# A batch's closing chain of attention, done within the two batches behind it

## The reference

```python
x = x + attn_a(layernorm(x))     # linear layer, cumulative sum over the features
x = x + ffn(layernorm(x))        # 8 experts, the 2 best for each token
x = x + attn_b(layernorm(x), ...)
x = x + ffn(layernorm(x))

def attn_b(x, Wq, bq, Wk, bk, Wv, bv, Wo, bo):      # 16 heads of 8 features
    q, k, v = x @ Wq.T + bq, x @ Wk.T + bk, x @ Wv.T + bv
    scores = einsum('bqhd,bkhd->bhqk', q, k) / sqrt(8)
    scores = where((j <= i) & (j >= i - 128), scores, -10000.0)   # i query, j key
    attn = softmax(scores) + 1e-9
    return einsum('bhqk,bkhd->bqhd', attn, v) @ Wo.T + bo
```

## Time and profile before

| | us |
|---|---|
| median of 3 runs | 1003.95 (993.8 to 1005.53) |
| the profiled execution | 1002.63 |
| its span, first to last instruction | 1000.6 |
| PE busy / DVE busy / ACT busy in the span | 686.4 / 645.7 / 407.8 |
| stage of attn_b | about 369 to 716 |
| mean granted clock of PE | 0.865 of full |

### The profile page before, as it was taken

One profiled execution on the slowest core, in us unless ns is written; L12 is line 12 of the kernel. 1 busy time (PEld: TensorE's weight loads), 2 busy tenths in 40 slices (PEclk: granted clock), 3 DMA queues, 4 the chain that ended last, 5 costly groups with the idle time before them and its releaser, 6 DMA issues.

```text
span 1000.6 us, 29220 instructions
## 1 busy us (share of the span) xinstructions
PE 686.4 (69%) x10592; PEld 511.6 (51%) x10592; DVE 645.7 (65%) x2608; ACT 407.8 (41%) x691; POOL 437.5 (44%) x413
## 2 busy tenths in 40 slices
PE   3811777797667677885978879867675668566780
PEld 2511566675546553553545555555465556455660
DVE  7887887864444569764668576777778634354444
ACT  1370245353333332753547447555354234233340
POOL 6591573584655500213031100051486766666661
PEclk9999967999887796997899889987759999789895
DMA  7210012132212220111111101001011111223114
GB/s 223 59 32 3 25 35 67 49 68 56 62 51 85 67 79 26 55 56 37 53 28 60 51 24 58 4 3 44 17 51 49 43 44 41 64 75 104 54 41 137
DMA packets 62921, 54.53 MB, mean 54 GB/s; under 512 B 10129, under 2 KB 55954, under 8 KB 62778
## 3 DMA queue, kind: packets, MB, share of 16 engines
q1 hardware_dynamic: 53250, 33.12, 11.2%
q0 software_dynamic: 9536, 19.55, 7.8%
HBM read 31.79 MB, written 20.84 MB: 53 GB/s over the span
## 4 chain that ended last, share of the span: by engine, by line
PE 38%; DVE 30%; issue 12%; another core or an unknown queue 7%; DVEq 4%; DMA 3%; ACT 3%; SPq 1%; POOL 1%; ACTq 0%; POOLq 0%
PE stbank L1115 6%; DVE sbank L830 4%; PE stbank L1102 4%; PE stbank L1104 3%; PE stbank L1116 3%; DVE gl L770 3%; DVE zr L589 3%; PE bank L1209 3%; PE sbank L1167 2%; PE stbank L1103 2%; DVE ysb L760 2%; DVE st L560 2%; PE stbank L1193 2%; DVE xs L786 2%
## 5 line engine op out<-in xcount | busy, mean ns | idle before, releaser
L479 POOL DMA_INDIRECT xg<-table,idx x156 | 160.5, 1029 | 168.2 <-PE sbank L1083 58.7
L909 ACT ACTIVATE g<-stbank 128x512 f32<-128x512 f32 x156 | 93.3, 598 | 322.0 <-PE stbank L1104 235.6
L1115 PE MATMUL stbank<-wff,gh 128*128 x624 | 142.1, 306 | 112.2 <-DVE ysb L760 70.7
L434 POOL TENSOR_TENSOR r<-ve,mhalf 128x4 f32<-128x4 f32 (+1 forms) x32 | 43.1, 1346 | 305.6 <-DVE ve L566 211.2
L760 DVE TENSOR_REDUCE ysb<-stbank 128x128 f32<-128x256 f32 x156 | 65.9, 422 | 153.2 <-remote 90.4
L1102 PE MATMUL stbank<-xT,wff 128*128 128x128 f16 x624 | 149.6, 247 | 18.1 <-issue 12.3
L1104 PE MATMUL stbank<-xT,wff 128*128 128x128 f16 x624 | 149.8, 247 | 0.5 <-issue 0.4
L1103 PE MATMUL stbank<-xT,wff 128*128 128x128 f16 x624 | 147.2, 243 | 0.0
L956 ACT ACTIVATE pT<-stbank 128x1024 f32<-128x1024 f32 (+1 forms) x128 | 116.6, 915 | 74.2 <-PE stbank L1193 73.9
L1115 PEld LDWEIGHTS stbank<-wff,gh 128*128 128x128 f16 x624 | 67.2, 108 | 145.4 <-issue 128.2
L830 DVE CUSTOM_DVE_ANT_0 sbank<-sbank,mskew 128x160 f32<-128x160 f32 x384 | 113.2, 356 | 27.0 <-PE sbank L1167 26.7
(11 more groups left out here) (187 smaller groups left out, 1366.2 us busy)
## 6 DMA issues: line engine op xcount, KB each, us to landing
yslot<-ysb SPq DMA_DIRECT2D x78, 64.0 KB
table<-tb SPq DMA_DIRECT2D x16, 256.0 KB
cg<-ytab SPq DMA_DIRECT2D x16, 256.0 KB
qz<-dumps SPq DMA_DIRECT2D x96, 32.0 KB
kst<-dumps SPq DMA_DIRECT2D x96, 32.0 KB
xg<-table,idx POOLq DMA_INDIRECT x156
xs<-in_x SPq DMA_DIRECT2D x8, 256.0 KB, 4.9
qz<-in_w SPq DMA_DIRECT2D x1, 2048.0 KB, 10.0
```

The lines of the kernel that those rows point to most:

```text
L479: g.indirect_dma_start(xg[:, i % G].rearrange("p a d -> p (a d)"), None, table[cc % 2], bass.IndirectOffsetOnAxis(ap=idx[:, cc % 2, t:t + ...
L909: a.activation(g32[:, i % 3, :], hbank[i % 2], ACT.Silu, scale=1.0 / WSCALE)
L1115: mm(o, gh[:, i % 3, P * f:P * f + P], whl, start=(f == 0), stop=False, skip_group_check=True)
```

## The change

- `back` is taken apart. Within iteration b, PE transposes `uT` of batch b-1 in slots 3, 7, 11 and 15 (`u_rows`), and DVE's division follows (`context`). The contexts of batch b-2 are transposed in slot 1 (`context_columns`, now into `bank[1]`), copied, and projected in slot 2 (`project`), then added (`add_attention`). What is left of batches 6 and 7 follows the loop.
- The row transposes go to bank 3 of `stbank`. For that the units with kt = 3 put their four heads side by side into one bank, and the band matmuls of kt = 1 and kt = 3 write the whole width, since the mask that had stayed in these banks is overwritten. In units with kt = 1 `scores_t` waits for the division.
- `uT` exists twice, for even and odd batches. The odd ones lie in buffers that the stage does not use otherwise.
- `FRONT_EARLY` is 2 instead of 4: every step of the preparation is two slots later, and batch 2's steps 2 and 3 are done in the loop.
- `max_rows(b, 1)`, which was at the end of the iteration, is in slot 0 of the next. The router's counts for cc = 2 are in `sbank` instead of `bank[1]`. Waits are adapted.

```diff
-FRONT_EARLY = 4
+FRONT_EARLY = 2
+CTX_AT = 1
...
+        uT = [[u_even[:, i, :] for i in range(SETS)],
+              [gh[:].rearrange("p a n -> p (a n)").bitcast(F32)[:, 0:SEQ], gl[:].rearrange("p a n -> p (a n)").bitcast(F32)[:, 0:SEQ],
+               g32[:, 2, :], ysb[:].rearrange("p a n -> p (a n)")]]
...
+        rbank = [bank[1][:, :] if cc != CHUNKS else sbank[:, 1, :] for cc in range(2 * CHUNKS)]
...
+        def u_bank(b, qt):
+            return stbank[:, TPB - 1 if b + 1 < B else qt, :]
...
             for b in range(B):
                 for j in range(UNITS):
                     if b + 1 < B:
                         reduce(b + 1, j)
+                    if j == CTX_AT + 1 and b >= 2:
+                        add_attention(b - 2)
+                    if b and j % TPB == TPB - 1:
+                        context(b - 1, j // TPB)
                     front_in_attention(front, b, j)
                     router_in_attention(r_step, b, j)
-                back(b)
+            add_attention(B - 2)
+            for qt in range(TPB):
+                context(B - 1, qt)
+            add_attention(B - 1)
...
                     if j >= 2:
                         exps(b, j)
+                    if j == 0:
+                        max_copy(b, 1)
+                    if j == CTX_AT and b >= 2:
+                        ctx_copy(b - 2)
...
             def front(b, j):
                 if j == 5:
-                    wait(pe, s_oa, b - 2)
+                    wait(pe, s_oa, b - 3)
...
                 if j == 0 and half == 0:
                     pe.wait_ge(s_stk[b % 2], 16 * 24 * (b // 2 + 1))
-                    wait(pe, s_cx, TPB * (b - 1))
...
                 wait(pe, s_e, UNITS * b + j - 1)
-                halves = 2 if kt < TPB - 1 else 1
-                for half in range(2):
-                    bank_ = stbank[:, 2 * (j % 2) + half, :].rearrange("p (g a n) -> p g a n", g=2, a=2)
+                if b and kt == 1:
+
+                    wait(pe, s_cx, TPB * (b - 1) + j // TPB)
+                w = 256 if kt < TPB - 1 else P
+                flat_ = stbank[:].rearrange("p a n -> p (a n)")[:, 1024 * (j % 2):1024 * (j % 2) + 4 * w]
+                for o in range(0, 4 * w, 512):
                     for c in range(NBLK):
                         r = slice(BLK * c, BLK * c + BLK)
...
+                        if kt in (0, 2):
+                            out_ = flat_[r, o:o + 512].rearrange("p (g a n) -> p g a n", g=2, a=2)[:, :, :, r]
+                            band = mband[:].rearrange("p (a n) -> p a n", a=2)[:, :, r].unsqueeze(1).to_broadcast([P, 2, 2, BLK])
+                        else:
+                            out_ = flat_[r, o:o + 512]
+                            band = mband[:, 0:w].unsqueeze(1).to_broadcast([P, 512 // w, w])
+                        mm(out_, ident16[:, r], band, start=True, stop=False, tile_position=(0, BLK * c), skip_group_check=True)
...
+            def u_rows(b, qt):
+                if qt == 0:
+                    pe.wait_ge(s_u, SETS * (b + 1))
+                dst = u_bank(b, qt)
+                for s in range(SETS):
+                    ins = pe.transpose(dst[:, P * s:P * s + P], uT[b % 2][s][:, P * qt:P * qt + P], ident[:])
+                ins.then_inc(s_ut, 1)
+
+            def context_columns(b, maxima):
+                pe.wait_ge(s_mt, maxima)
+                wait(pe, s_oa, b)
+                pe.wait_ge(s_cx, TPB * (b + 1))
                 for qt in range(TPB):
...
+                    ins = pe.transpose(bank[1][:, P * qt:P * qt + P], cx[:, qt, :], ident[:])
                 ins.then_inc(s_cxp, 1)
...
                         if j >= 2:
                             scores_t(b, j)
+                        if j == 0:
+                            max_rows(b, 1)
+                        if j == CTX_AT and b >= 2:
+                            context_columns(b - 2, 2 * (b + 1))
+                        if j == CTX_AT + 1 and b >= 2:
+                            project(b - 2)
+                        if b and j % TPB == TPB - 1:
+                            u_rows(b - 1, j // TPB)
                         front_in_attention(front, b, j)
...
-                back(b)
+            context_columns(B - 2, 2 * B)
+            project(B - 2)
+            for qt in range(TPB):
+                u_rows(B - 1, qt)
+            context_columns(B - 1, 2 * B)
+            project(B - 1)
```

More of the change, by code:

```diff
@@ L540, in _ @@
             layer_pass(a_step, r_step, x_step, beside, 0)
-            front(2, 2)
             for b in range(B):
@@ L824, in reduce @@
                 if j == 0:
+                    wait(dve, s_mtp, 2 * b - 1)
+                if j == MAX_SPLIT:
                     wait(dve, s_mtp, 2 * b)
@@ L832, in reduce, with context, add_attention @@
                     ins.then_inc(s_red, 1)
-            def back(b):
-                for qt in range(TPB):
-                    dve.wait_ge(s_ut, TPB * b + qt + 1)
-                    u = sbank[:, qt % 2, :].rearrange("p (h r) -> p h r", r=32)
-                    v.reciprocal(rden[:, qt, :], u[:, :, DK])
-                    dve.drain()
-                    v.tensor_tensor(cx[:, qt, :].rearrange("p (h j) -> p h j", j=DK), u[:, :, 0:DK],
-                                    rden[:, qt, :].unsqueeze(2).to_broadcast([P, NH, DK]), ALU.mult).then_inc(s_cx, 1)
+            def context(b, qt):
+                dve.wait_ge(s_ut, TPB * b + qt + 1)
+                if qt == 0:
+                    wait(dve, s_cxp, b)
+                u = u_bank(b, qt).rearrange("p (h r) -> p h r", r=32)
+                v.reciprocal(rden[:, qt, :], u[:, :, DK])
+                dve.drain()
+                v.tensor_tensor(cx[:, qt, :].rearrange("p (h j) -> p h j", j=DK), u[:, :, 0:DK],
+                                rden[:, qt, :].unsqueeze(2).to_broadcast([P, NH, DK]), ALU.mult).then_inc(s_cx, 1)
+            def add_attention(b):
                 dve.wait_ge(s_o, b + 1)
@@ L954, in exps @@
                 wait(act, s_pv, i - 2)
-                src = stbank[:, 2 * (j % 2):2 * (j % 2) + 2, :].rearrange("p a (g n) -> p (a g) n", g=2)[:, :, 0:w]
-                a.activation(pT[:, i % 3, 0:4 * w].rearrange("p (g n) -> p g n", g=4), src, ACT.Exp, scale=SCALE).then_inc(s_e, 1)
+                src = stbank[:].rearrange("p a n -> p (a n)")[:, 1024 * (j % 2):1024 * (j % 2) + 4 * w]
+                a.activation(pT[:, i % 3, 0:4 * w], src, ACT.Exp, scale=SCALE).then_inc(s_e, 1)
             def u_copy(b, s):
                 act.wait_ge(s_pv, UNITS * b + TPB * (s + 1))
-                wait(act, s_ut, TPB * b)
-                a.activation(uT[:, s, :], bank[0][:, :], ACT.Copy).then_inc(s_u, 1)
+                wait(act, s_ut, TPB * (b - 1))
+                a.activation(uT[b % 2][s], bank[0][:, :], ACT.Copy).then_inc(s_u, 1)
             def ctx_copy(b):
                 act.wait_ge(s_cxp, b + 1)
-                a.activation(cT, bank[0][:, :], ACT.Identity, bias=vsum[:, b % 3, :]).then_inc(s_ct, 1)
+                wait(act, s_o, b)
+                a.activation(cT, bank[1][:, :], ACT.Identity, bias=vsum[:, b % 3, :]).then_inc(s_ct, 1)
             def max_copy(b, part):
@@ L1068, in r_step @@
                         for i in range(2):
-                            ins = mm(IX, ohl_[:, i, t, :], oht[:, i, t, :], start=(t == 0 and i == 0),
+                            ins = mm(IX[cc], ohl_[:, i, t, :], oht[:, i, t, :], start=(t == 0 and i == 0),
                                      stop=(t == CT - 1 and i == 1))
@@ L1204, in pv @@
                     wait(pe, s_u, SETS * b + s)
-                    if s == 0:
-                        wait(pe, s_ct, b)
                 for g in range(4):
@@ L1218, in max_rows @@
                     pe.wait_ge(s_vsr, min(b + 2, B))
-                    wait(pe, s_oa, b - 1)
                 else:
@@ L1225, in max_rows, with project @@
                 ins.then_inc(s_mtp, 1)
-            def back(b):
-                pe.wait_ge(s_u, SETS * (b + 1))
-                for qt in range(TPB):
-                    if qt >= 2:
-                        pe.wait_ge(s_cx, TPB * b + qt - 1)
-                    for s in range(SETS):
-                        ins = pe.transpose(sbank[:, qt % 2, P * s:P * s + P], uT[:, s, P * qt:P * qt + P], ident[:])
-                    ins.then_inc(s_ut, 1)
-                for qt in range(TPB):
-                    pe.wait_ge(s_cx, TPB * b + qt + 1)
-                    ins = pe.transpose(bank[0][:, P * qt:P * qt + P], cx[:, qt, :], ident[:])
+            def u_rows(b, qt):
+                if qt == 0:
+                    pe.wait_ge(s_u, SETS * (b + 1))
[7 more added lines that the diff above has]
+                pe.wait_ge(s_cx, TPB * (b + 1))
+                for qt in range(TPB):
+                    ins = pe.transpose(bank[1][:, P * qt:P * qt + P], cx[:, qt, :], ident[:])
                 ins.then_inc(s_cxp, 1)
-                pe.wait_ge(s_mt, 2 * min(b + 2, B))
+            def project(b):
```

(4 more changed lines are left out.)

50 lines of the change are left out of this document (20 added, 30 removed).

## The result

| | before | changed |
|---|---|---|
| median (lowest to highest), us | 1000.37 (993.8 to 1005.53) | 1012.79 (1009.91 to 1016.23) |
| changed / before | | 1.0127, 95% interval 1.0076 to 1.0178 |
| profiled execution, span | 1000.6 | 1014.5 |

The account below looks back on a forecast made before the run. TensorE bounds the inside of a batch, nothing the boundaries, where one chain passes between PE, DVE and ACT. 50.1 + 2.7 - 13 - 7 - 9 - 4 - 3.5 + 8 = 24.3 us off 1002.6: 979 us, 8-in-10 range 960 to 1000.

Parts of the forecast that it names:

- Part 1: Batch boundaries: spreading the attention's chain over the next batch's slots wins all their idle time and lost clock, 50.1 us.
- The rival of the returning stalls: Boundary stalls without a cause, 13.2 us, belong to the program's flow and come back: 992 us, chance 0.10.
- an idle 2.3 us on DVE in mid-batch: Sign that the forecast is wrong: the boundary's stalls without a cause show up inside a batch.
- Part 2: Fronts two slots later: batch 2's statistics and normalisation leave the loop ahead of batch 0, 2.7 us gained.
- part 6: SP's queue: row maxima wait behind the stack loads, uncovered in batches 0 and 1, 4 us lost, range nothing to 16.
- Part 3: Wider band matmuls for kt = 1 and 3, four column tiles side by side: 1.9 us a batch, 13 us lost.
- the rival of no overlap: Band matmuls of 512 columns on column tiles run one by one, 9.5 us a batch: 1032 us, chance 0.06.
- Parts 4 and 5: Turns between whole-array and column-tile matmuls, 7 us lost; TensorE idle in slots 0 and 1 behind DVE, 9 us lost.
- PE's wait for the maxima's row in batches 0 and 1 alone: Sign that the forecast is right: only these two batches lack cover for SP's queue, 2 us each.
- Part 7: Tail behind batch 7: batch 6's columns and projection come before batch 7's row transposes, 3.5 us lost.
- band groups at 0.4 us: Sign that the forecast is right: kt = 1 band groups take 0.4 to 0.5 us to the next start.
- no idle time of TensorE over 3 us at a boundary: Sign that the forecast is right: no stretch of a batch boundary has PE idle for over 3 us.

Follow-up runs that it names:

- e2: Kernel before without GpSimd's indirect gathers for batches 4 to 7 in the second stage's attention, condition A: 972.18 us, ratio 0.9811.
- condition B: Label of the three run groups in which the kernel before took 917.2, 915.0 and 916.6 us.
- e10: Kernel before, unchanged, run for its profile in condition B: 914.2 us.
- e1: Changed kernel without GpSimd's indirect gathers for batches 4 to 7 in the second stage's attention, condition A: 975.78 us, ratio 0.9845.
- e11: Kernel before with the fronts two slots later alone (FRONT_EARLY 2 for 4), no chain moved, condition B: 956.52 us, ratio 1.0471.
- e9: Changed kernel as it is, beside the kernel before in condition B: 921.57 us, ratio 1.0071.
- e16: Kernel before with the band layout alone (512 columns for kt = 1 and 3), gathers as they were, condition B: median 917.2 us, ratio 0.9987.
- e4: Changed kernel with the row maxima's store and load ahead of SyncE's last stack loads, condition A: 1003.27 us, ratio 1.0115.
- e8: Changed kernel with gathers one per two slots and the row maxima's store and load ahead of SyncE's last stack loads, condition B: 922.18 us, ratio 1.0057.
- e15: Kernel before with the fronts two slots later and the row maxima's store and load ahead of SyncE's last stack loads, condition B: 946.18 us, ratio 1.0292.
- condition A: Label of the run groups in which the kernel before took 991.5 and 998.4 us, as it did for the result.

## Why the prediction was wrong

**Part 1, the step that failed.** "That is all the change can win there, for the chain's own matmuls are done as before, only elsewhere" took every idle us and every slow clock in the stretches as the chain's, and all of it, 50.1 us, as gained. Cut at the exponentials, boundaries 0-5 of the kernel before hold 47.6 us of idle time and lost clock (busy x (1 - clock), as in the prediction). Without gathers they hold 21.7 (e2), in condition B 22.0 (e10). So 26 us went with the burst, and the burst moved along: its new place made slots 0-5 28 us longer, among dense TensorE work. Nor did the rest go: without gathers the changed kernel still has 16.6 us of it at its boundaries (e1). They are 29.2 us shorter than in e2 because 25.6 us of busy TensorE moved into the slots, where idle time, 12.1 us before and 4.2 after, took up only 7.9.

The changed kernel whose gathers don't stand in a row takes 975.8, 975.7 and 976.5 us, close to the 979 of the forecast. That is luck: the sum's gain held 26 us of the burst, bands priced at 13 us cost 2 or nothing, the lead and the tail cost more than was said, and the kernel before took 991.5 and 998.4 us beside these runs, not the 1002.6 that the sum started from.

The rows had the hint: the POOL column of the earlier trace rows shows 7 to 9 us in four boundaries, and 1.04 and nothing in the two from 586 and 624 us; these two were the short ones, 15.9 and 12.9 us from exponential to exponential against 17.2 to 26.5. The stall of the earlier trace rows stood inside a burst of 458.9 to 468.8 us, and 2.30 us in the earlier trace rows at the end of one.

**The rival of the returning stalls** had the right event and the wrong mechanism. It was priced at 13.2 us with a chance of 0.10, and "the program's flow" was the only mechanism in it; e1 rules that one out. The stalls belonged to GpSimd's queue, whose move the text didn't follow. Its sign "an idle 2.3 us on DVE in mid-batch" came as 19.8 us in four waits.

**Part 2.** 2.7 us gained was wrong in sign: the lead takes 25.6 us in e10 and e2, and 27.4 with the fronts later (e11), 27.5 in e1. And the fronts two slots later, of which this part and part 6 see 2.7 us gained and 4 lost, cost the kernel before 40 us by themselves in condition B. Taken in that order the rest of the change gives back 35 of them (956.5 us in e11, 921.6 in e9).

**Part 3.** The price of a band group was right. Two groups of the changed kernel, kt = 1 and kt = 3, each with what follows:

```profile
509.59 0.62 PE L1216 MATMUL stbank<-mband,ident 128*32 128x512 f16 x8
510.02 0.46 PE L1221 MATMUL stbank<-qz,kst 128*32 128x160 f16 x16
...
512.47 0.40 PE L1216 MATMUL stbank<-mband,ident 128*32 128x512 f16 x4
512.69 0.38 PE L1221 MATMUL stbank<-qz,kst 128*32 128x128 f16 x16
```

0.43 and 0.22 us to the next start, 0.43 and 0.21 forecast, at a granted clock of 1.00: eight times 512 columns one by one are 1.71 us at 2.4 GHz, and 1.71 / 0.43 = 3.97 tiles at once. By an estimate from the 3.07 that the Trainium skill, TensorE: Matmul & The Clock Gate, section Measured speedup vs the span model, has for four row tiles, it would have been 0.56 us; the measurement decides. The sum over a batch wasn't paid (e16): the rival of no overlap is out, and so are most of the 13 us.

**Parts 4 and 5** were not measured alone. With clean slots they show together in busy TensorE: 29.4 us a batch before (19.59 + 9.80), 30.9 changed (24.49 + 6.38), 1.5 more where parts 3 and 4 had 3.1; idle TensorE falls from 5.7 to 3.1 us where part 1 gave back 5.1, and 2.4 of clock. A clean batch goes from 35.1 to 34.0 us, not from 40 to 35.

**Part 6.** The wait for the maxima row came in nearly every batch, 10.7 us in seven, so the sign "PE's wait for the maxima's row in batches 0 and 1 alone" was wrong:

```profile
507.46 5.64 SPq L353 DMA_DIRECT2D kst<-dumps  x12
513.14 0.30 SPq L380 DMA_DIRECT2D mdump<-mT  x1
...
516.92 0.41 PE L1216 MATMUL stbank<-mband,ident 128*32 128x128 f16 x8 [2.22 <-DMA qz<-mdump]
```

What it costs stays open: with 3 us of it taken away, 1 us came off in e4 and none in e8, both within the noise, and 7 to 8 us of it stayed. In the kernel before with its fronts delayed, the same mend is worth 10 us by the medians and 16 by the ratios (e11, e15).

**Part 7.** The tail takes 14.6 us for 8.3, 6.3 more where 3.5 were said, and 13.9 to 15.2 in every changed kernel. Two chains stand behind each other there, the first addition to x at 718.44 and the second, of 0.69 us, at 727.12, with the whole row transposes between:

```profile
715.93 1.12 PE L1270 MATMUL bank<-bo_s,ones_row 1*128 1x512 f32 x2 [0.78 <-ACT g L982]
...
718.44 0.69 DVE L854 TENSOR_TENSOR xs<-xs,bank 128x512 f32<-128x512 f32 x1 [1.96 <-PE bank L1273]
...
723.76 1.32 PE L1270 MATMUL bank<-bo_s,ones_row 1*128 1x512 f32 x2 [0.78 <-ACT g L982]
...
727.12 0.69 DVE L854 TENSOR_TENSOR xs<-xs,bank 128x512 f32<-128x512 f32 x1 [4.91 <-PE bank L1273]
```

Batches 6 and 7, which the text counted with 4.9 us gained, give nothing: slots +3.9 and +4.0, boundary -5.2.

**Signs that came true:** band groups at 0.4 us; no idle time of TensorE over 3 us at a boundary, which the kernel before doesn't have without gathers either (1.2 us at most in e2); a batch of 33 to 34 us where no burst stands. The granted clock is 1.00 there from batch 2 on, but 0.89 in batches 0 and 1 even without gathers (e1).

## What to carry to other kernels

Idle time that no semaphore explains has a cause beside the engines on the path: list what every queue does in the stretch, GpSimd's too, and look for a sibling stretch that lacks it. When an edit moves a step that releases another queue, ask where that queue's work lands. Spread indirect DMAs over the slots instead of issuing them in a row: here one wait was worth 28 us to the changed kernel in condition A (1.0127 to 0.9847; 37 by the 0.9757 of a group in which the kernel before was slower), 10 us to the kernel before, and in condition B it cost that kernel 6 us. Price a step that is moved by itself: the fronts' two slots, priced as a small gain, cost the kernel before 40 us alone.

## What the runs showed of the hardware

- Eight indirect gathers in a row (0.95 us each, 0.30 apart) made TensorE, VectorE and ScalarE stand without a releaser in condition A (ScalarE 38.7 us in five waits); one per two slots took the changed kernel no longer than none (975.7 and 975.8 us). The Trainium skill, Runtime: NRT & Kernel Launch, section Instruction fetch mechanics, has the cost of crossing into the next 16 KB page of instructions as mostly hidden. The runs without stalls agree, with a page every 5.2 to 5.4 us; in A none of these pages came for 13 to 20 us around seven of the two kernels' eight bursts. That this is the cause is not shown.
- The same program took 991.5 to 1000.4 us in some groups and 915.0 to 917.2 in others, by the medians. Of the 89 us between the two profiles, 30 lie ahead of the stage of attn_b and 32 behind it; the 27 inside it are the bursts' but for 3 (345.6 us, 321.4 without gathers, 318.3 in B). Part of the time behind lies in TensorE's idle time with nothing to wait for in the expert layer, where GpSimd issues indirect DMAs all along. Ahead of the second matmul of the experts, 715 to 910 us, kernel before in A, then in B, which is further on at 910 us:

```profile
L1115 PE MATMUL stbank<-wff,gh 128*128 x212 | 48.3, 307 | 42.6 <-DVE ysb L760 24.7 <-issue 17.6
```

```profile
L1115 PE MATMUL stbank<-wff,gh 128*128 x272 | 54.6, 281 | 12.3 <-DVE ysb L760 11.7
```

What sets the condition is not known, nor that the indirect DMAs cause the idle time outside the stage; a verdict on a kernel with gathers holds for the condition in which it was taken.
